# Attention values with the padded values held still and the turned weights moving, as four column tiles

## What is computed

```python
# layer 1: v is the context itself; layer 3: q, k, v are projected, and there is an output projection
scores = q @ k^T / sqrt(.)            # per image and head: 128 x 77, with a mask
attn   = softmax(scores, axis=-1)
x      = attn @ v                      # per image and head: 128 x 77 times 77 x 8
```

## Time and profile before

| | |
|---|---|
| median of 3 executions | 783.5 us (776.53, 783.5, 801.49) |
| the profiled execution | 781.5 us, its span 779.8 us |
| PE, PEld busy | 692.8 us (89%), 542.7 us (70%) |
| DVE, ACT, POOL busy | 482.2 us (62%), 431.2 us (55%), 208.5 us (27%) |
| mean granted clock of TensorE | 0.928 |
| chain that ended last | PE 69%, DVE 17%, ACT 6%, issue 3%, POOL 3% |
| matmuls of the values | 512 records, 63.6 us busy |

### The profile page before, as it was taken

The page is one execution under the profiler, slowest core; times in us unless marked ns, Lnnn a source line. Parts: engine busy times, 40 slices in busy tenths (PEclk is TensorE's granted clock), DMA queues, the critical chain, the costliest instruction groups (busy, mean ns, idle before and its releaser), DMA issues.

```text
span 779.8 us, 9948 instructions
## 1 busy us (share of the span) xinstructions
PE 692.8 (89%) x3452; PEld 542.7 (70%) x3459; DVE 482.2 (62%) x1092; ACT 431.2 (55%) x803; POOL 208.5 (27%) x215
## 2 busy tenths in 40 slices
PE   5889999998997999889899989857589999689997
PEld 1689987887665767667676767634358897567775
DVE  2476665575566574575547456468925552388996
ACT  4366556645367577483584757232145441787873
POOL 3333004831140232243324111130016211115531
PEclk9699999998999999999999999867889996699999
DMA  5111002110002000120202000100001000100000
GB/s 129 47 46 40 1 1 69 31 53 1 0 14 67 14 28 7 61 80 15 68 11 72 1 0 1 44 0 0 2 0 55 1 2 0 28 27 28 2 1 27
DMA packets 27360, 20.97 MB, mean 27 GB/s; under 512 B 5409, under 2 KB 22571, under 8 KB 27311
## 3 DMA queue, kind: packets, MB, share of 16 engines
q1 hardware_dynamic: 26591, 20.29, 8.6%
q10 hardware_dynamic: 720, 0.04, 0.1%
HBM read 19.80 MB, written 0.52 MB: 26 GB/s over the span
## 4 chain that ended last, share of the span: by engine, by line
PE 69%; DVE 17%; ACT 6%; issue 3%; POOL 3%; DMA 1%; ACTq 0%; DVEq 0%; POOLq 0%
PE PS L1442 61%; PE PS L1663 3%; PE PS L1548 2%; PE PS L1463 1%; ACT XN L737 1%; ACT H1h L827 1%; PE PS L1599 1%; DVE SN L1124 1%; DVE H2l L1166 1%; DVE H1l L1166 1%; POOL WL L628 1%; ACT PS L830 1%; DMA GW<-in_L_gate_T 1%; DVE ST L998 1%; DVE QS L1301 1%
## 5 line engine op out<-in xcount | busy, mean ns | idle before, releaser
L628 POOL TENSOR_TENSOR WL<-RAW,WH 128x512 fp32r<-128x512 f32 (+2 forms) x76 | 89.2, 1191 | 149.9 <-ACT WH L721 149.6
L1166 DVE TENSOR_TENSOR H2l<-PS,H2h 128x512 fp32r<-128x512 f32 x72 | 49.0, 688 | 64.3 <-ACT PS L830 64.0
L620 POOL TENSOR_TENSOR RSTD<-VE,MHALF 128x4 f32<-128x4 f32 x18 | 19.3, 1074 | 197.2 <-DVE VE L1008 161.5
L1442 PE MATMUL PS<-H1h,WH 128*128 128x512 f32 x146 | 61.5, 421 | 6.9 <-DVE H1l L1166 6.9
L1442 PEld LDWEIGHTS PS<-V,ATT 77*128 77x128 f32 x512 | 65.2, 198 | 1.0 <-issue 0.6
L1442 PE MATMUL PS<-XTh,WH 128*128 128x512 f32 x128 | 55.5, 434 | 11.3 <-DVE XTl L1026 6.0
L1246 DVE TENSOR_REDUCE MX<-PS 128x4 f32<-128x308 f32 x64 | 30.6, 478 | 55.0 <-PE PS L1442 54.9
L646 POOL TENSOR_TENSOR XT<-XT,YW 128x512 f32<-128x512 f32 x24 | 32.2, 1343 | 118.2 <-DVE YW L1103 118.2
L1442 PE MATMUL PS<-V,ATT 77*128 77x9 f32 x512 | 63.6, 251 | 0.0
L845 ACT ACTIVATE ATT<-ATT 128x308 f32<-128x308 f32 x64 | 29.4, 459 | 57.3 <-DVE ATT L1254 57.2
L721 ACT ACTIVATE ATT<-PS 77x512 f32<-77x512 f32 (+5 forms) x76 | 38.3, 518 | 39.3 <-PE PS L1834 18.5
(11 more groups left out here) (248 smaller groups left out, 1770.3 us busy)
## 6 DMA issues: line engine op xcount, KB each, us to landing
RAW<-in_L_ffn_spec_W SPq DMA_DIRECT2D x4, 1024.0 KB, 5.6
RAW<-in_L_ffn_w SPq DMA_DIRECT2D x16, 256.0 KB, 3.0
RAW<-in_L_ffn_up_W SPq DMA_DIRECT2D x8, 256.0 KB, 2.7
RAW<-in_L_ffn_down_W SPq DMA_DIRECT2D x8, 256.0 KB, 3.4
RAW<-in_L_ffn_spec1a_W SPq DMA_DIRECT2D x2, 512.0 KB, 4.0
RAW<-in_L_ffn_spec1b_W SPq DMA_DIRECT2D x2, 512.0 KB, 5.1
RAW<-in_L_ffn_wg SPq DMA_DIRECT2D x4, 176.0 KB, 2.7
RAW<-in_L_ffn_wu SPq DMA_DIRECT2D x4, 176.0 KB, 2.7
```

What stands on the lines that cost most here:

```text
L620: step(g.tensor_tensor(RSTD[:, c], VE[:, c], MHALF[:, c], ALU.pow))
L628: g.tensor_tensor(lo, RAW[0:r["rows"], r["raw"] + s["c0"]:r["raw"] + s["c1"]], hi.bitcast(fp32), ALU.subtract).then_inc(lo_done, 1)
L1166: v.tensor_tensor(lo, full, hi.bitcast(fp32), ALU.subtract).then_inc(split_done, 1)
L1442: return t_.matmul(o, l, r, start=start, stop=stop)
```

## The change

The two operands of the value matmul change places. `V1` is copied by POOL, for each image, into `VR`, where each head has DV = 32 columns (nine of them filled, the others zero), double-buffered. A head's matmul holds VR's 77 x 32 still and moves PT's 77 x 128; head m of the group writes to partitions 32m to 32m+31, which makes four column tiles of the array. An image's output is then turned (a head's 32 rows by 128 tokens, a group in each quarter of the bank). ACT copies the bank to `OT`, and PE turns it back with four 128 x 128 transposes into the same bank (`values_back`, BACK_LAG = 7), and `weighted` waits for that (WEIGH_LAG becomes 9). The loops get two steps more. POOL gets, for each image, the copy to VR, which from the third image on waits until the values two images earlier are done (`o_full`), a memset of VR ahead of each attention, and the waits that this memset needs.

```diff
+        VR = ATT3[0:KC, 0:2 * NH * DV].rearrange("k (s h d) -> k s h d", s=2, h=NH)
+        OT = ATT3[:, 3072:4096]
...
@@ POOL, head_keys(layer, kt, some): after the keys of image b
+                    if b >= first + 2:
+                        pool.wait_ge(o_full, b - 1)
+                    g.tensor_copy(VR[:, b % 2, :, 0:DK + 1], V1[:, b - first, :].rearrange("k (h d) -> k h d", h=NH)
+                                  ).then_inc(values_ready, 1)
@@ POOL, order of the stream
             pool.wait_ge(split_done, LAST0["hid"])
+            pool.wait_ge(y0_full, 2)
+            step(g.memset(VR[:, :, :, :], 0.0))
             head_keys(1, CT, range(2))
             rstd(5)
             head_keys(1, CT, range(2, 5))
             for k in range(4):
                 pool.wait_ge(row_high, k + 1)
-                pool.wait_ge(bdk_ready, 5)
+                pool.wait_ge(values_ready, 5)
...
             pool.wait_ge(k3_ready, 2)
+            pool.wait_ge(v3_ready, 2)
+            pool.wait_ge(f2_added, B)
+            step(g.memset(VR[:, :, :, :], 0.0))
             head_keys(3, K3T, range(2))
             rstd(14, 15)
@@ ACT, attention
-                for i in range(B * NG + EVAC_LAG):
+                for i in range(B * NG + BACK_LAG - 1):
+                    b = first + (i - VALUE_LAG - NG) // NG
+                    if b >= first and (i - VALUE_LAG) % NG == 0:
+                        act.wait_ge(o_full, b + 1)
+                        c = slice((b % 2) * HALF, (b % 2 + 1) * HALF)
+                        copy(OT[:, c], PS[6 + b % 2][:, :]).then_inc(ot_ready, 1)
@@ DVE, weighted(b)
-                    dve.wait_ge(o_full, b + 1)
-                    o = PS[6 + b % 2][:, 0:NH * (DK + 1)].rearrange("p (h d) -> p h d", h=NH)
+                    if b > first:
+                        dve.wait_ge(o_done, b)
+                    dve.wait_ge(back_full, b + 1)
+                    o = PS[6 + b % 2][:, :].rearrange("p (h d) -> p h d", h=NH)
@@ PE, values(g)
+                    if g % NG == 0:
+                        pe.wait_ge(values_ready, b + 1)
+                    c = slice((g % NG) * S, (g % NG + 1) * S)
                     for m in range(GH):
-                        h = (g % NG) * GH + m
-                        c = slice(h * (DK + 1), (h + 1) * (DK + 1))
                         at = (g % 3) * HALF + m * S
-                        last = mm(PS[6 + b % 2][:, c], PT[:, at:at + S], V1[:, t, c])
+                        last = mm(PS[6 + b % 2][m * DV:(m + 1) * DV, c], VR[:, b % 2, (g % NG) * GH + m, :], PT[:, at:at + S])
@@ PE, new, and its loop
+                def values_back(b):
+                    pe.wait_ge(ot_ready, b + 1)
+                    for k in range(NG):
+                        at = (b % 2) * HALF + k * S
+                        last = t_.transpose(PS[6 + b % 2][:, k * GH * DV:(k + 1) * GH * DV], OT[:, at:at + S], ident[:, :])
+                    last.then_inc(back_full, 1)
+
-                for i in range(B * NG + VALUE_LAG):
+                for i in range(B * NG + BACK_LAG):
...
-                    if i >= VALUE_LAG:
+                    if VALUE_LAG <= i < B * NG + VALUE_LAG:
                         values(g0 + i - VALUE_LAG)
+                    b = first + (i - BACK_LAG) // NG
+                    if b >= first and (i - BACK_LAG) % NG == NG - 1:
+                        values_back(b)
...
-TURN_LAG, EVAC_LAG, VALUE_LAG, WEIGH_LAG = 3, 3, 5, 7
+TURN_LAG, EVAC_LAG, VALUE_LAG, BACK_LAG, WEIGH_LAG = 3, 3, 5, 7, 9
+DV = 32
```

More of the change, by code:

```diff
@@ L470, in program @@
         pt_full, pt_act, pt_dve, o_full, o_done = sem("pt_full"), sem("pt_act"), sem("pt_dve"), sem("o_full"), sem("o_done")
+        values_ready, ot_ready, back_full = sem("values_ready"), sem("ot_ready"), sem("back_full")
         ont_full, ont_ready, wo_full = sem("ont_full"), sem("ont_ready"), sem("wo_full")
@@ L834, in attention @@
                 g0 = first * NG
-                for i in range(B * NG + EVAC_LAG):
+                for i in range(B * NG + BACK_LAG - 1):
[4 more added lines that the diff above has]
+                        copy(OT[:, c], PS[6 + b % 2][:, :]).then_inc(ot_ready, 1)
                     g = g0 + i - EVAC_LAG
-                    if g >= g0 and g % NG != NG - 1:
+                    if g0 <= g < g0 + B * NG and g % NG != NG - 1:
                         act.wait_ge(pt_full, g + 1)
```

## The result

The changed kernel takes 793.51 us in the median of four runs (793.04 to 794.37); the kernel before took 783.92 beside it (four runs, 776.53 to 801.49). The ratio is 1.0155, with a 95% interval of 1.0085 to 1.0226: slower, by about 12 us by this ratio, where 33 were forecast. The profiled execution took 793.2 us, its span is 791.3 against 779.8.

A forecast was written before the change was run, and what follows sets the result against it. PE bounds the kernel, 1.98 us a group in steady state. Groups +7, POOL's places +3, +9, +6, ends +4, clock +5 make 34 us on 781.5, plus 2 for the median: 817 us, range 793 to 839.

The forecast's parts named there:

- the 0.56 us for the values: A group's eight value records on PE: forecast 0.56 us where the old ones took 0.89, overlapping only in pairs.
- the rival: All four tiles side by side: values 0.23 us a group, body -14 us, time 796 us; chance 0.22.
- The bound 0.23: Lower bound for a group's values on PE: all four tiles beside each other, two records and a little issue, 0.23 us.
- Switches: PE changing the array's partition around each group's values: 0.13 us going in, 0.20 coming out, 0.33 for both.
- The turn back: Four PE transposes an image, 0.44 us or 0.11 a group; ACT's copy of 0.60 hidden in steady state.
- POOL's three places: Where PE waits for POOL: layer 1's attention start +3.0 us, image 5 +9.0, layer 3's attention start +6.0.
- First scores: Start of layer 1's attention: keys wait for y0_full and the memset, +3.0 us.
- Image 5: Layer 1, scores 20: row splits, strips and keys queue behind the copy for image 4; PE stands still, +9.0 us.
- Layer 3's entry: Start of layer 3's attention: memset, two images' keys and copies between f2_added and rstd, +6.0 us.
- The clock: The two new stalls each bring a stretch of granted clock 0.50, 2.5 us each, +5 us.
- The ends: Behind each attention's last values: +1.4 us in layer 1, +2.6 in layer 3, together +4.0.
- the other terms: The 27 us of the forecast sum that don't depend on the values: POOL's waits, the ends and the clock.

The follow-up runs named there:

- tiles_0011: The changed kernel with a group's four heads on two column tiles, later heads overwriting earlier ones, division by constants; 809.71 us, one run.
- full_width: The changed kernel without column tiles: the padded V of four heads held as one 77x128 operand, division by constants; 810.84 us, ratio 1.0435.
- pool_only: The kernel before with only POOL's part of the change (memsets, copies to VR, their waits) and the old values on PE; 826.77 us, ratio 1.0618.
- by_need_old_values: The kernel before with POOL's and ACT's work in the order PE needs, plus POOL's memsets and copies, old values; 776.93 us, ratio 0.9968.
- work_by_need_2: Second run of keys_late3 with layer 1's POOL work, and the row splits' ACT copies, in the order PE needs; 766.45 us, ratio 0.9834.
- keys_late3: keys_first with layer 3's first keys moved between the two root steps of its entry; 774.56 us, ratio 0.9975.
- keys_first: The changed kernel with POOL building keys before copies and memsets, and layer 3's first keys and root steps before its memset; 776.73 us, ratio 0.9964.

## Why the prediction was wrong, step by step

**The step that failed** is the 0.56 us for the values: "if records start in program order, the next head's first can only run beside this head's second". They don't wait for one another. The two records of a head do lie behind each other, 0.134 us apart, but only for their own tile; the other tiles' first records start 7 ns apart. The values take two records' time, as the rival had it. A group is 1.64 and not 2.09 - 0.11 = 1.98, an image 6.96 and not 8.36, and over sixteen images that is 22 us, all but 1 of the 23.5 between 817 and 793.5. That rival's own time was 796. The bound 0.23 was read rightly, and its rival had a chance of 0.22; the choice between the bounds was made by an argument about a queue for which no row stood. The Trainium skill, TensorE: Matmul & The Clock Gate, Measured speedup vs the span model, states about one matmul plus 4 ns for each further tile; the starts 6 to 7 ns apart agree in kind. I had put its neighbour statement, on program order, above it; the trace of tiles_0011 doesn't agree with that one, as head 2's first record starts 0.013 us behind head 0's and ahead of head 1's.

**Switches** held. Forecast 0.13 in and 0.20 out, 0.33; measured 1.64 - 1.09 = 0.55 for values and switches together, of which two records and their starts are 0.23 to 0.26, so 0.29 to 0.32. The Trainium skill, TensorEngine Tiling (Array Packing), Key Properties, has TensorE drained at a change of mode; the waits of 0.16 and 0.20 us before the loads, absent in full_width, agree.

**The turn back**: forecast 0.44 an image, measured 2.04 - 1.64 = 0.40. ACT's copy was hidden.

**POOL's three places** were seen rightly, with their causes, and sized a little low. First scores +3.8 (forecast 3.0): PE's idle time ahead of them grew from 0.32 to 3.52, 3.2 us for memset, keys and semaphores, and the other 0.6 were there before, as the last matmul ahead of it starts at 118.73 and not 118.14. Image 5: a wait of 10.4 us (forecast 9.3 beyond a wait of 0.3). The block behind the copy was 15.7 us where 15.8 was reckoned; the copy came at 155.24, not 150.9, since everything was later. Layer 3's entry: the shift goes from 16.6 us at 568.21 (584.80 after) to 23.9 at the first mask (580.34 and 604.22), 7.3 (forecast 6.0). Counted from f2_added to the end of ACT's scaling it is 10.6 us against 4.6, the 6.0 of the forecast; behind it the query products at the lower clock add 1.8 (3.78 against 1.98 us), which the forecast had under the clock.

**The clock** was forecast at +5 as if every stall cost its own stretch. The stall at image 5 did cost 2.8 us more (two groups of 3.02 in place of 1.64), the start of the attention 1.5 (3.35 for the first group, not 1.81), the early mixture 3.3 (its shift is 21.2 us at 466.33, which is 487.54 after). But the new values hold or regain the full clock where the old ones didn't. Behind the last scores of layer 3 it stays at 1.00 for 4.9 us in the kernel before, for 8.9 in pool_only and for 10.6 and 10.7 in the two kernels with the old values and the order of need, but for 18 us or more in all nine that move 128 columns. The ends, forecast at +4, cost about 3 in layer 1 and gave back 7.0 in layer 3 (18.5 to 11.5). Not all of the 7.0 is the values' doing: 5.0 of it, up to the projection, is there with the old values too once POOL's order is changed (10.37 us from last scores to projection, 10.33 with the new values, 15.23 in the kernel before); between by_need_old_values and work_by_need_2 3.1 are left. pool_only shows the stall without this help.

**Not foreseen**: the keys of layer 3 moved away from DVE's work, which gave 3.5 us back (keys_late3 against keys_first shows the cause). And the gain of 15.6 us wasn't all to be had. Between the first and the last scores of a layer 6.6 us of it were due (an estimate: 26 groups' values at 0.345, less 0.4 for each of six turns back). Layer 3 has 5.4 of them, since PE waits 1.41 us for keys behind three strips, up to 616.64, and 0.28 before. Layer 1 has about 2.9, when stall and clock are taken out; groups 7, 8 and 10 alone, where ACT is at 13.7 of 16 us, take 0.5 to 0.7 longer each than in work_by_need_2.

So the other terms, 27 us in the forecast, did come to 11.5 + 15.6 = 27.1, but by chance. By the landmarks they are: POOL 3.8 + 9.9 + 7.3 = 21.0; half clock, the early mixture and layer 1's end 2.8 + 1.5 + 3.3 + 2.8 = 10.4; gains that don't arrive between the scores 15.6 - 5.4 - 2.9 = 7.3; less 3.8 from there to layer 2, 0.8 in layer 2 and 7.0 at the end.

The time lies at the lower end of the range of 793 to 839, and its ratio of 1.0155 within the 2% to which 0.23 was given. Slower was forecast and came out; the loss was forecast nearly three times too large, by the one term of the values.

## What to carry to other kernels

Price a piece of work on an in-order engine by what is queued behind its wait, not by its length: sixteen copies of 0.32 us and two memsets cost 46 us in one place and nothing in another. A faster stage can only arrive earlier at a wait that is set elsewhere, so put the engine's stream in the order of need first, then make the stage faster: 784 to 794 us without, 777 to 766 with. And where a term has two bounds and no row between them, a rung in the middle is no estimate; it has to be argued from a row, or both ends carried.

## What the runs showed of the hardware

- float32 matmuls of 32 weight columns on four column tiles run at once although each is two records: 0.35 us from load to load for eight, 0.56 on two tiles, 0.99 on one.
- Two tiles' records start independently: in tiles_0011 the first ones start 0.013 us apart, though the program has three records of the first tile between them.
- A switch from full to 32-column operands and back costs about 0.30 us: a group takes 2.28 us with all four heads on one tile and 1.98 at full width, the eight records being equally long.
- At the lower clock PE can be busy for 32.00 of 32 us and stay there (pool_only, old values, nine moving columns), while the same attention with 128 moving columns was back at full level about 6 us after the stall's end, with column tiles (changed kernel) and without them (full_width).
- A DVE operation beside a POOL multiplication ended with it: TENSOR_SCALAR 0.18 us alone, 2.06 beside the keys, ending at 520.63 where POOL's first keys ended at 520.60; the next, 0.69 alone, took 2.29, to 0.5 us past the second keys. In the changed kernel a TENSOR_SCALAR of the statistics, 0.17 alone, took 2.11 beside the keys at 589.30, hidden behind POOL's own chain. The Trainium skill, Trainium Architecture — The Big Picture, What this means for kernel authors, says that DVE and GpSimd share one pair of ports with an exclusive lock; the traces agree for these operations, while RECIPROCAL, between the first two and beside the second keys, took 0.35 as it does alone.
